# A tile of every other bucket fetched row by row from SyncE and ScalarE, with SyncE's joins and loads run ahead

## The reference

```
h = relu(layernorm(x))
values = exp(sum(h[src]@K.T * relations[rel] * h[src]@Q.T) / 128)     # per edge
values = values / (sum of values over the edges with the same (src, rel))
msgs   = values * h[dst]                                               # per edge
output = segment_sum(msgs, (src, rel))                                 # [16, 6250, 128]
W[r]   = sum_b comps[r,b] * bases[b]                                   # 16 matrices 128 x 128
x + relu(sum_r output[r] @ W[r])
```

## Time and profile before

| | |
|---|---|
| median of 3 runs | 3081.46 us (3079.8 to 3084.72) |
| the profiled execution | 3066.26 us, span 3064.5 us |
| busy: PE / DVE / ACT / POOL | 1549.4 / 1354.7 / 462.7 / 1651.2 us |
| mean granted clock of TensorE | 0.673 of full speed |
| DMA | 170.47 MB, 56 GB/s mean |

### The profile page before, as it was taken

The page is one execution under the profiler, slowest core; times in us unless marked ns, Lnnn a source line. Parts: engine busy times, 40 slices in busy tenths (PEclk is TensorE's granted clock), DMA queues, the critical chain, the costliest instruction groups (busy, mean ns, idle before and its releaser), DMA issues.

```text
span 3064.5 us, 32426 instructions
## 1 busy us (share of the span) xinstructions
PE 1549.4 (51%) x9121; PEld 1129.2 (37%) x9122; DVE 1354.7 (44%) x2385; ACT 462.7 (15%) x918; POOL 1651.2 (54%) x1804
## 2 busy tenths in 40 slices
PE   4999932444344454534454443544444444544435
PEld 3666621233233333323333332333333333333324
DVE  7999934334243433424343342434334243433423
ACT  4666611000010100001010000101000010101000
POOL 3444444655646465555646565564655556464653
PEclk8999965656666665666666566666656566666667
DMA  5444411111111111111111111111111111111111
GB/s 154 156 155 155 155 55 32 46 41 42 45 36 45 36 46 39 43 42 41 45 36 45 38 44 43 40 45 37 45 38 43 44 39 45 36 46 36 45 42 29
DMA packets 99825, 170.47 MB, mean 56 GB/s; under 512 B 32491, under 2 KB 48612, under 8 KB 99575
## 3 DMA queue, kind: packets, MB, share of 16 engines
q0 software_dynamic: 51776, 104.48, 13.1%
q1 hardware_dynamic: 47672, 65.57, 6.3%
q10 hardware_dynamic: 352, 0.14, 0.0%
HBM read 112.24 MB, written 59.59 MB: 56 GB/s over the span
## 4 chain that ended last, share of the span: by engine, by line
another core or an unknown queue 40%; issue 21%; DVE 20%; PE 14%; SPq 2%; DMA 2%; DVEq 1%; ACT 0%; POOLq 0%; ACTq 0%
PE bank L1199 6%; DVE arena L825 4%; DVE CX L790 3%; PE bank L1184 2%; DVE stage L768 2%; DVE WC L801 2%; DVE pay_all L784 1%; PE bank L1152 1%; PE bank L1276 1%; DVE OHR L766 1%; PE bank L1319 1%; DMA RL<-bucket_streams 1%; DVE pay_all L815 1%; PE bank L1307 1%
## 5 line engine op out<-in xcount | busy, mean ns | idle before, releaser
L492 POOL DMA_INDIRECT arena<-Z_messages,IDX x1568 | 1483.0, 946 | 1137.4 <-issue 955.1
L1319 PE MATMUL bank<-arena 128*128 128x128 f32 x3528 | 695.2, 353 | 733.1 <-issue 724.9
L1319 PEld LDWEIGHTS bank<-arena 128*128 128x128 f32 x3528 | 632.5, 264 | 797.3 <-issue 795.3
L799 DVE TENSOR_SCALAR WC<-bank 128x128 f32<-128x128 f32 x49 | 14.3, 292 | 1150.5 <-remote 1149.2
L1101 ACT COPY pay_all<-bank 128x1024 bf16<-128x1024 bf16 x147 | 108.0, 807 | 2136.6 <-remote 2059.9
L1307 PE MATMUL bank<-pay_all 128*128 128x256 bf16 x882 | 179.8, 347 | 310.9 <-DVE arena L825 249.1
L825 DVE TENSOR_TENSOR arena<-stage,bank 128x512 f32<-128x512 bf16 x441 | 268.9, 681 | 12.1 <-remote 7.8
L768 DVE TENSOR_TENSOR stage<-bank,NLF 128x4608 bf16<-128x4608 f32 x49 | 242.4, 4948 | 0.0
L1307 PEld LDWEIGHTS bank<-pay_all 128*128 128x128 bf16 x882 | 86.6, 113 | 386.2 <-DVE arena L825 297.4
L1276 PE MATMUL bank<-stage,OHR 128*128 128x512 bf16 (+1 forms) x441 | 198.5, 618 | 3.2 <-DVE arena L825 3.1
L1199 PE MATMUL bank<-WT,HT 128*128 128x512 f32 x392 | 186.3, 615 | 0.0
(11 more groups left out here) (211 smaller groups left out, 1715.5 us busy)
## 6 DMA issues: line engine op xcount, KB each, us to landing
Z_messages<-stage SPq DMA_DIRECT2D x192, 256.0 KB
arena<-Z_messages,IDX POOLq DMA_INDIRECT x1568
X<-in_x SPq DMA_DIRECT2D x4, 768.0 KB, 12.8
out<-O SPq DMA_DIRECT2D x48, 64.0 KB
bucket_streams<-bucket_streams SPq DMA_DIRECT2D x97, 18.0 KB
arena<-in_L_gnn_bases_w SPq DMA_DIRECT2D x1, 1024.0 KB, 15.0
bucket_streams<-arena SPq DMA_DIRECT2D x1, 882.0 KB
RL<-bucket_streams SPq DMA_DIRECT2D x49, 18.0 KB
```

The costliest lines, as they stand in the source:

```text
L492: g.indirect_dma_start(Gbuf[par][:, k, :], None, Z, bass.IndirectOffsetOnAxis(IDX[turn][:, k:k + 1], 0))\
L1319: return t_.matmul(bank[2][:, 0:EMB], OW[:, k, :], Gbuf[par][:, k, :], start=start, stop=stop)
```

## The change

**SyncE.** Both joins of bucket b+1 are started before the records of b are loaded, and SyncE no longer waits for those records to land; it no longer stores the output. In odd buckets it also loads one row of 128 records (tile ROWK = 1 of the bucket, `ONER`), and then fetches rows 32 to 127 of that tile of bucket b-2: for each eight rows one load of eight row numbers into registers (line 350), and eight transfers of one row of `Z_messages` (512 bytes) into one partition (line 354), 96 transfers. Each adds 16 to the semaphore `row`. These wait for `onez`, for `acc` >= (its bucket) - 1 and `shared` likewise.
**ScalarE.** `shared_tile(b)` moves from `bucket(b)` to `bucket(b+1)`, behind the copies and `spread_relations`. Behind it stand the output's store and, in odd buckets, rows 0 to 31 of tile 1 in the same manner (lines 1126, 1130).
**GpSimd.** In the 24 odd buckets tile 1 is left out: 29 fixed gathers instead of 30. Its waits are the same.
**VectorE.** In odd buckets it waits for `ONER` and makes the row numbers (two instructions on one partition, `ONEZ`) ahead of `IDX`; one more step in the making of the counts.
**TensorE and `shared_tile`** wait for `row` in odd buckets.

```diff
--- before.py
+++ after.py
...
+        ROWK = 1
+        ACTROWS = 32
+        ROWS = 16 * P
...
-                def bucket(b, par, rl_total):
-                    if dyn(b) or b < NB:
-                        sp.wait_ge(s["join"], b * 32 + 16)
+                def load_one(b, turn, m):
+                    if dyn(b) or m >= 1:
+                        sp.wait_ge(s["onez"], m * 2 - 1)
                         sp.sem_inc(s["sp_go"], 1)
-                        if dyn(b) or 1 <= b < NB - 1:
-                            join(b + 1, 0)
-                            sp.wait_ge(s["join"], b * 32 + 32)
-                            sp.sem_inc(s["sp_go"], 1)
-                        if dyn(b) or b >= 2:
-                            sp.wait_ge(s["rl_t"], b - 1)
-                            sp.sem_inc(s["sp_go"], 1)
-                        load_records(b, par)
-                    if dyn(b) or b + 1 < NB:
-                        sp.wait_ge(rl[par], rl_total)
+                    row = sp.value_load(ROWI[0:1, bass.ds(b + 5 * NB + 1, 1)], min_val=0, max_val=(TOP + E) // P)
+                    sp.dma_start(ONER[turn][:], stream[bass.ds(row + ROWK, 1), :]).then_inc(oner[turn], 16)
+                def single_rows(b, turn, m):
+                    sp.wait_ge(s["onez"], m * 2 + 2)
+                    sp.sem_inc(s["sp_go"], 1)
+                    if dyn(b) or b >= 3:
+                        sp.wait_ge(s["acc"], b - 1)
+                        sp.wait_ge(s["shared"], b - 1)
+                    sp.sem_inc(s["sp_go"], 1)
+                    for p in range(ACTROWS, P, 8):
+                        _, rows = nc.values_load_multi_w_load_instructions(
+                            ONEZ[turn][:, 1, p:p + 8], engines=[mybir.EngineType.SP], min_val=0, max_val=ZROWS - 1,
+                            skip_runtime_bounds_check_because="a record holds a row of Z or the empty row")
+                        for k in range(8):
+                            sp.dma_start(Gbuf[1][p + k:p + k + 1, ROWK, :], Z[bass.ds(rows[k], 1), :]).then_inc(s["row"], 16)
+                def bucket(b, par, turn=None, m=None):
+                    sp.wait_ge(s["join"], b * 32 + 16)
+                    sp.sem_inc(s["sp_go"], 1)
+                    if dyn(b) or 1 <= b < NB - 1:
+                        join(b + 1, 0)
+                        sp.wait_ge(s["join"], b * 32 + 32)
                         sp.sem_inc(s["sp_go"], 1)
-                        if not dyn(b) and b == 0:
-                            join(1, 0)
-                            sp.wait_ge(s["join"], 32)
-                            sp.sem_inc(s["sp_go"], 1)
                         join(b + 1, 1)
                     if dyn(b) or b >= 2:
-                        store_out(b - 2, par)
-                def store_out(b, par, n=P):
-                    sp.wait_ge(s["o"], b + 1)
-                    sp.dma_start(out[bass.ds(b * P, n), :], O[par][0:n, :]).then_inc(ost[par], 16)
+                        sp.wait_ge(s["rl_t"], b - 1)
+                        sp.sem_inc(s["sp_go"], 1)
+                    load_records(b, par)
+                    if par == 1:
+                        load_one(b, turn, m)
+                    if par == 1 and (dyn(b) or b >= 3):
+                        single_rows(b - 2, 1 - turn, m - 1)
+                    if not dyn(b) and b == 0:
+                        sp.wait_ge(rl[0], 16)
+                        join(1, 0)
+                        sp.wait_ge(s["join"], 32)
+                        join(1, 1)
                 join(0, 1)
-                bucket(0, 0, 16)
-                bucket(1, 1, 16)
-                with sp.Fori(0, (NB - 1) // 2 - 1) as j:
-                    bucket(j * 2 + 2, 0, j * 16 + 32)
-                    bucket(j * 2 + 3, 1, j * 16 + 32)
-                bucket(NB - 1, 0, None)
-                store_out(NB - 2, 1)
-                store_out(NB - 1, 0, LASTN)
+                bucket(0, 0)
+                bucket(1, 1, 0, 0)
+                with sp.Fori(0, (NB - 3) // 4) as j:
+                    bucket(j * 4 + 2, 0)
+                    bucket(j * 4 + 3, 1, 1, j * 2 + 1)
+                    bucket(j * 4 + 4, 0)
+                    bucket(j * 4 + 5, 1, 0, j * 2 + 2)
+                for b in range(2 + (NB - 3) // 4 * 4, NB):
+                    bucket(b, b % 2, b // 2 % 2, b // 2)
+                single_rows(NB - 2, (NB - 2) // 2 % 2, (NB - 2) // 2)
...
                     for k in range(FIRSTK, FLOOR):
-                        tile(k)
+                        if par == 0 or k != ROWK:
+                            tile(k)
...
+                    if turn % 2 == 1:
+                        dve.wait_ge(oner[turn // 2], one_total)
+                        v.tensor_copy(ONEZ[turn // 2][:, 0, :], ONER[turn // 2][:]).then_inc(s["onez"], 1)
+                        dve.wait_ge(s["onez"], m * 2 + 1)
+                        v.tensor_scalar(ONEZ[turn // 2][:, 1, :], ONEZ[turn // 2][:, 0, :], 7, None, ALU.logical_shift_right)\
+                            .then_inc(s["onez"], 1)
...
-                def shared_tile(b, par):
+                def store_out(b, par, n=P):
+                    act.wait_ge(s["o"], b + 1)
+                    act.sem_inc(s["act_go"], 1)
+                    a.dma_start(out[bass.ds(b * P, n), :], O[par][0:n, :]).then_inc(ost[par], 16)
+
+                def single_rows(b, turn, m):
+                    act.wait_ge(s["onez"], m * 2 + 2)
+                    act.sem_inc(s["act_go"], 1)
+                    if dyn(b) or b >= 3:
+                        act.wait_ge(s["acc"], b - 1)
+                        act.wait_ge(s["shared"], b - 1)
+                    act.sem_inc(s["act_go"], 1)
+                    for p in range(0, ACTROWS, 8):
+                        _, rows = nc.values_load_multi_w_load_instructions(
+                            ONEZ[turn][:, 1, p:p + 8], engines=[mybir.EngineType.Activation], min_val=0, max_val=ZROWS - 1,
+                            skip_runtime_bounds_check_because="a record holds a row of Z or the empty row")
+                        for k in range(8):
+                            a.dma_start(Gbuf[1][p + k:p + k + 1, ROWK, :], Z[bass.ds(rows[k], 1), :]).then_inc(s["row"], 16)
+
+                def shared_tile(b, par, row_total):
 
                     last = act.value_load(ROWI[0:1, bass.ds(b + 6 * NB + 1, 1)], min_val=0, max_val=G - 1)
                     g_total = act.value_load(ROWI[0:1, bass.ds(b + (1 + par) * NB, 1)], min_val=16 * (FLOOR - PACED), max_val=16 * G * (NB + 1) // 2)
                     act.wait_ge(gat[par], g_total)
                     act.sem_inc(s["act_go"], 1)
+                    if par == 1:
+                        act.wait_ge(s["row"], row_total)
...
                         spread_relations(b + 1, 1 - par)
-                        shared_tile(b, par)
+                    if dyn(b) or b >= 1:
+                        shared_tile(b - 1, 1 - par, m * ROWS)
+                    if dyn(b) or b >= 2:
+                        store_out(b - 2, par)
+                    if par == 1:
+                        single_rows(b, turn, m)
...
-                def aggregate(b, par):
+                def aggregate(b, par, row_total):
...
                     pe.sem_inc(s["pe_go"], 1)
+                    if par == 1:
+                        pe.wait_ge(s["row"], row_total)
```

More of the change, by code:

```diff
@@ L187, in program @@
         IDX = [sb(f"IDX{p}", [P, G], I32) for p in range(4)]
+        ONER = [sb(f"ONER{p}", [1, P], F32) for p in range(2)]
+        ONEZ = [sb(f"ONEZ{p}", [1, 2, P], I32) for p in range(2)]
         NLI = sb("NLI", [P, 2, G], I32)
@@ L215, in program @@
             h th ht so_mm so_sb prod z_mm z_sb zst0 zst1 zrow v ends ends_mm nt nt_total nt_mm nt_row shared act_go join sp_go marks_sb marks_st
-            rl0 rl1 rl_t ri dec nlf idx inv rrf ohn ohr ord vr cnt cm cx cs masks x3 w w3 bd tp oht lk ow gat0 gat1 land0 land1 land2 land3 acc o ost0 ost1
+            rl0 rl1 rl_t ri dec nlf idx inv rrf ohn ohr ord vr cnt cm cx cs masks x3 w w3 bd tp oht lk ow gat0 gat1 land0 land1 land2 land3 oner0 oner1 onez row acc o ost0 ost1
             pool_go pe_go iota_p
@@ L231, in program @@
         XB = [(NB - 1) * k // 4 for k in range(5)]
+        oner = [s["oner0"], s["oner1"]]
+        ROWK = 1
+        ACTROWS = 32
+        ROWS = 16 * P
         def over_t(ap, n):
@@ L713, in _ @@
             chain(v.scalar_tensor_tensor(out=col(6), in0=col(1), scalar=-1.0, in1=col(6), op0=ALU.add, op1=ALU.add), "nt")
+            chain(v.tensor_tensor(col(6), col(6), PARI[:, 1:2], ALU.subtract), "nt")
             chain(v.tensor_tensor(col(3), col(6), PARI[:, 1:2], ALU.mult), "nt")
@@ L769, in tables, with gather_index @@
                         .then_inc(s["ohn"], 1)
-                def gather_index(b, turn):
+                def gather_index(b, turn, m, one_total):
                     dve.wait_ge(s["ri"], b + 1)
@@ L835, in finish, with stepb @@
                         .then_inc(s["o"], 1)
```

(44 more changed lines are left out.)

## The result

The changed kernel takes 3764.51 us (3762.1 to 3770.28) where the kernel before takes 3080.63: ratio 1.222, 95% interval 1.220 to 1.224. It is 684 us slower; the forecast was 360 slower and the range ended at 3680. On four of the five chips used later the kernel before takes 3067 to 3081 us. On the fifth it takes 2394 us, and two close relatives of the changed kernel save 29 us (see e5 to e8); the changed kernel itself was not run there.

What follows compares the result with a forecast made beforehand. GpSimd gathering or waiting was taken to fill each bucket's cycle, with SyncE's rows lengthening the pauses. 3066.3 − 30 + 70 − 5 + 332 = 3434, + 15 = about 3448, rounded down to 3440 us; range 3040 to 3680.

Steps and rivals of the forecast that it cites:

- B: The forecast itself: SyncE's single-row transfers are the bound and lengthen the pause, 3440 us; chance 0.45.
- Item 1: GpSimd issues one gather less in 24 odd buckets: −30 us, if the pause stays as it is.
- item 2: Shared tile one bucket later: the next gather waits for ScalarE's copy, +1.5 us a pause, 47 pauses, +70 us.
- items 3 and 4: SyncE running ahead with its record loads, −5 us (bounds 0 and −15); output stores moved to ScalarE, 0.
- item 5: SyncE's row transfers: 375 steps needed a pair of buckets, 290 supplied, 85 made up in the pause, +332 us.
- The need: SyncE's steps per pair of buckets for rows, row-number loads, joins and record loads: 375.
- The price of 1.2 us a step: SyncE's step beside gathers, read from twelve slow steps in 14.3 us: 27 steps in 32 us a bucket.
- D: Rival: ScalarE's rows come first and make its copies late in odd buckets, +120 us, 3236; chance 0.08.
- A: Rival: SyncE's rows fit beside the gathers and cost nothing, 3116 us, at most 3151; chance 0.22.
- C: Rival: SyncE's early joins and loads bring TensorE's results sooner, 8.3 us less pause a cycle, 3033 to 2925; chance 0.20.
- the upper bound of the supply: SyncE's steps at 1.4 us over the whole gather time: 177 lacking a pair, +692 us, 3808; chance 0.07.

Runs made afterwards that it cites:

- e5: Changed kernel without one-row transfers, tile 1 gathered again in all buckets, shared tile copied in its own bucket; 2394.06 us, kernel before 2393.66 on that chip.
- e8: Changed kernel with 48 of the single rows on ScalarE and 80 on SyncE; 2364.19 us, ratio 0.9877 to the kernel before (2393.66) on that chip.
- e3: Changed kernel with SyncE fetching 72 of its 96 rows, the other 24 left out of the computation; 3464.67 us, ratio 1.1258 to the kernel before.
- e4: Changed kernel with each eight one-row transfers of SyncE made one transfer of eight neighbouring rows at a fixed place; 3286.89 us, ratio 1.0681 to the kernel before.
- e6: Kernel before without the gather of tile 1 in odd buckets (left out of the computation); 2363.14 us, ratio 0.9874 to the kernel before (2393.66).
- e1: Kernel before with one edit, the shared tile copied one bucket later; 3144.75 us, ratio 1.0217 to the kernel before.
- e2: Changed kernel without one-row transfers on SyncE and ScalarE, GpSimd gathering tile 1 again in all buckets; 3143.26 us, ratio 1.0211 to the kernel before.
- e7: Changed kernel with ScalarE's 32 rows left out, SyncE's 96 kept; 2364.43 us, ratio 0.9877 to the kernel before (2393.66) on that chip.
- e14: Kernel before with one register load on GpSimd ahead of each gather; 2892.28 us, ratio 0.944 to the kernel before.
- e15: Kernel before with three register loads on GpSimd ahead of each gather; 3916.85 us in its one run.
- e17: Changed kernel with one register load on GpSimd ahead of each gather; 3454.37 us, ratio 1.1292 to the kernel before.
- e18: Kernel before with one semaphore increment on GpSimd ahead of each gather; 3103.98 us, ratio 1.0123 to the kernel before.
- e13: Kernel before with each gather fetching 64 of its 128 rows, the rest left out of the computation; 3081.64 us, ratio 1.0047 to the kernel before.
- e11: Changed kernel without ScalarE's 32 rows, on a chip like the first; 3730.48 us, ratio 1.2106 to the kernel before.
- e16: Changed kernel with each of SyncE's 96 one-row transfers replaced by three increments of an unawaited semaphore; 3297.81 us, ratio 1.0751 to the kernel before.

## Why the prediction was wrong

- **The sign and the mechanism held (B).** The row steps of odd buckets are SyncE's bound (e3, e4), they are made up in the pause, and `aggregate` waits for them. Item 1 (e6, on the chip without pauses), item 2 (e1: +67 for +70), items 3 and 4 together (e2: 0 for −5) were right to a few us.
- **The step that failed is the supply in item 5**: "the first 8 us at 0.17, 47 steps; [...] 12 us of the pause at 0.17, 71 steps". I count SyncE's records in 21 pairs of buckets of the changed kernel. The first 8 us of the gathers give 22 and 25 steps, not 47 each: the slow stretch begins 1.3 to 5.0 us after the first gather, mostly at about 4, and in every other pair SyncE also waits some 1.4 us for a join to land. That is 47 steps short, × 0.17 = 8 us a pair. Beside the rest of the gathers it makes 49 steps instead of 54, 0.8 us. And from the last row to the next gather it is 12.2 us, 10.4 of them `aggregate`; in these SyncE makes 53 of 72 possible steps, since it has only joins and the next load to do: 3.3 us. Together 12 us; the long pause was forecast at 13.9 + 1.5 + 14.4 = 29.8 us and measured at 42.7. The need, 375 steps, was right: 376 were counted. These 12.9 us, × 23 pairs, are 297 us of the miss.
- **A term that the sum left out: the last odd bucket.** Its rows have no later gathers to hide beside. They lengthen the stretch behind the last gather by 28 us. 297 + 28 = 325 us, about the distance from 3440 to 3764.5.
- **The price of 1.2 us a step was luck in part.** It was read as twelve slow steps in 14.3 us, but the trace has 18 records of SyncE in these 14.3 us, 11 long and 7 short, 0.8 us each, and the need was counted in records of either length. In the changed kernel it came out near 1.2 all the same: 26 steps in 30 us beside the gathers of an odd bucket, 1.15 us each; 23 in 32 beside those of an even one, in which ScalarE works too, 1.4 us.
- **What ScalarE's rows cost (D) was set at 0** because SyncE's shortage covers it. It does; alone it is 6.6 us in each long pause (e4), some 150 us in all.
- **A (the rows fit)** is what e7 and e8 show on their chip, and nowhere else did it come. There leaving the gathers out is worth 1.2%.
- **C did not occur.** In e2, with SyncE ahead, the weights still came 5.5 us after the last gather. What does bring them earlier is a stop of GpSimd's own (e14, e15, e17: all 46 begin while gathers are under way). C had the sign of e14 but named the wrong engine.
- **The range was too narrow**, since I took the upper bound of the supply (+692, 3808) as unlikely for its rate of 1.4 us a step; the rate was 1.15 to 1.4, but nearly the same time came about through steps that were not made and through the end.

What stays open: why the steps of SyncE and ScalarE take 0.70 us beside the gathers on four of the five chips of e1 to e18 and not on the one of e5 to e8. On such a chip GpSimd's register loads ahead of the gathers take them away (e14 has fewer, e15 none), by the distance that they make or by something else. It is neither the number of rows under way, down to half (e13), nor for the most part the other queue's steps (e11), nor the starting of transfers by the slow engine (e16). How short a stop between gathers would do was not tried: e18's increment made none.

## What to carry to other kernels

Price a sequencer's work in steps, and take the price from a stretch in which the same neighbour is busy: a transfer that costs 0.5 us alone cost 3 to 4 us beside indirect gathers. When one queue's work is to fit beside another's, count what it can do in each stretch of the cycle up to the moment from which its result is needed, not to the end of the cycle, and count the last cycle by itself. And time a change that moves work between queues on more than one chip.

## What was not expected of the hardware

- The same kernel took 3067 to 3081 us on four chips and 2394 on a fifth, with the gathers at 0.944 us on both kinds. On the fifth no step of SyncE's row transfers took over 0.28 us; on the others they took up to 1.4 us beside the gathers.
- With three register loads of GpSimd ahead of each gather none of SyncE's 1653 steps took 0.65 us or more, where 26 to 36% of them did in the kernel before.
- One register load of GpSimd ahead of each gather made the kernel before 5.6% faster on such a chip (2892 us), three made it 28% slower (one run). What the single load costs on a chip without slow steps was not tried.
- A gather of 64 rows took 0.908 us, one of 128 rows 0.944.
